# A three-stage graph layer on one core: bias in the mixing matrix, denominators among the last y products, edges six steps later, zeros from another tile

## The reference, cut to what matters

```python
xn = layernorm(x)                                  # 10,000 nodes x 512
agg = segment_sum(xn[src], dst) / max(deg, 1)      # 10,000 edges
h   = tanh(agg @ W1_l.T + xn @ W1_r.T + b1)
agg2 = segment_sum(h[src], dst) / max(deg, 1)
gnn = agg2 @ W2_l.T + h @ W2_r.T + b2
q, k, v = split(xn @ w_qkv)                        # 8 heads of 64
qp, kp = elu(q @ proj) + 1, elu(k @ proj) + 1
z   = 1 / (qp . sum_n kp)                          # one number per node and head
mix = (qp @ (kp^T v) * z) @ w_proj + b_proj
x   = x + gnn + mix
x   = x + ffn(layernorm(x))      # 8 experts, each node takes its best one
```

## Time and profile before

| | |
|---|---|
| median of 3 runs | 2788.45 us (2784.39 to 2789.29) |
| profiled execution | 2787.47 us, of which span 2785.7 us |
| mean granted TensorE clock | 0.975 |
| PE busy | 2614.7 us (94%) |
| DVE / ACT / POOL busy | 1698.5 / 987.7 / 1150.9 us |
| stage 1, first transpose to the last matmul | 26.8 to about 1022 us |
| fold and hidden | 1022 to 1519 us |
| mix, to the last product | 1519 to 2174 us |
| hand over to FFN, FFN | 2174 to 2786 us |

### The profile page before, as it was taken

How to read it: one execution, slowest core, us unless ns; L and a number is a source line. 1 busy time by engine, 2 the same in 40 slices (tenths; PEclk the granted TensorE clock), 3 DMA queues, 4 the chain that set the end, 5 groups by cost and what they waited for, 6 DMA issues and landing times.

```text
span 2785.7 us, 36335 instructions
## 1 busy us (share of the span) xinstructions
PE 2614.7 (94%) x11712; PEld 2080.2 (75%) x11712; DVE 1698.5 (61%) x3626; ACT 987.7 (35%) x1725; POOL 1150.9 (41%) x1089
## 2 busy tenths in 40 slices
PE   4899999999999989999998699999999699999999
PEld 3688888888888868888886366666667477777777
DVE  2677777777777744444443455555554477777774
ACT  2455554444444434444443222222221123223232
POOL 3577776666666630000000666666666111111110
PEclk7899999999999999999999899999999799999999
DMA  9566666455555555655665688888887323233231
GB/s 377 174 185 184 188 172 167 125 154 128 151 128 141 137 165 202 237 221 220 225 226 200 208 249 272 236 241 266 245 242 203 128 91 133 94 109 117 90 136 46
DMA packets 140309, 502.45 MB, mean 180 GB/s; under 512 B 27288, under 2 KB 27800, under 8 KB 99776
## 3 DMA queue, kind: packets, MB, share of 16 engines
q1 hardware_dynamic: 104384, 417.15, 40.2%
q0 software_dynamic: 35840, 84.23, 16.7%
HBM read 261.60 MB, written 239.73 MB: 180 GB/s over the span
## 4 chain that ended last, share of the span: by engine, by line
PE 70%; POOL 10%; issue 9%; DMA 4%; DVE 4%; ACT 1%; SPq 1%; POOLq 0%; ACTq 0%; DVEq 0%
PE bank L1158 55%; PE bank L1209 8%; POOL agg_d L360 3%; PE bank L1165 3%; POOL m_x L688 2%; DMA agg_d<-O,eidx 2%; POOL G_low L313 2%; POOL G L345 2%; DVE x2T_low L313 2%; PE bank L1345 2%; DMA agg_d<-O 1%; SPq L467 1%; PE bank L401 1%; PE bank L402 1%; ACT f_relu L847 1%
## 5 line engine op out<-in xcount | busy, mean ns | idle before, releaser
L313 POOL TENSOR_TENSOR G_low<-G,G_high 128x512 fp32r<-128x512 f32 x160 | 211.2, 1320 | 342.9 <-ACT G_high L423 342.9
L360 POOL DMA_INDIRECT agg_d<-O,eidx x160 | 273.2, 1707 | 70.1 <-issue 37.6
L345 POOL DMA_INDIRECT G<-y_d,esrc x80 | 83.3, 1041 | 494.4 <-DMA erow<-in_dst 481.9
L1005 DVE TENSOR_TENSOR m_x<-bank,m_x 128x512 f32<-128x512 f32 x80 | 55.3, 692 | 289.6 <-POOL m_x L688 263.3
L705 POOL TENSOR_SCALAR veps<-mv 128x1 f32<-128x1 f32 x80 | 26.9, 336 | 494.9 <-DVE mv L1050 494.9
L826 ACT CAST qz_high<-low 128x512 fp32r<-128x512 f32 x80 | 49.7, 621 | 395.1 <-DVE low L1018 263.7
L381 DVE SCALAR_TENSOR_TENSOR Sj<-erow,dstf,tri 128x128 f32<-128x128 int32 x160 | 162.3, 1014 | 35.5 <-DMA agg_d<-O 28.7
L390 DVE SCALAR_TENSOR_TENSOR eidx<-cnt,todump,dstf 128x1 int32<-128x1 f32 x160 | 176.6, 1104 | 8.0
L423 ACT CAST G_high<-G 128x512 fp32r<-128x512 f32 x160 | 98.9, 618 | 215.5 <-DVE G L921 196.7
L1158 PE MATMUL bank<-xnT_high,Wq_high 128*128 128x512 f32 x320 | 125.6, 393 | 28.4 <-DVE xnT_low L313 28.4
L661 POOL TENSOR_TENSOR bias<-bias,low 128x512 f32<-128x512 f32 (+1 forms) x80 | 143.5, 1794 | 0.0
(11 more groups left out here) (196 smaller groups left out, 7807.6 us busy)
## 6 DMA issues: line engine op xcount, KB each, us to landing
agg_d<-O SPq DMA_DIRECT2D x20, 1040.0 KB, 19.4
b_agg<-agg_d SPq DMA_DIRECT2D x20, 1040.0 KB, 8.4
a_x<-in_x SPq DMA_DIRECT2D x20, 1024.0 KB, 6.8
agg_d<-z_halves SPq DMA_DIRECT2D x20, 1024.0 KB, 5.7
q_d<-q_rows SPq DMA_DIRECT2D x80, 256.0 KB, 2.4
r_d<-r_rows SPq DMA_DIRECT2D x80, 256.0 KB, 3.7
r_in<-r_d SPq DMA_DIRECT2D x20, 1024.0 KB, 4.8
hT_high_d<-hT_made_high SPq DMA_DIRECT2D x20, 1024.0 KB, 10.3
```

The costliest lines, as they stand in the source:

```text
L313: return eng.tensor_tensor(out_, full, high.bitcast(F32), ALU.subtract)
L345: pool.indirect_dma_start(G[:, j, :], None, table, bass.IndirectOffsetOnAxis(ap=esrc[:, b, j:j + 1], axis=0)).then_inc(e_g[j], 16)
L360: pool.indirect_dma_start(agg, bass.IndirectOffsetOnAxis(ap=eidx[:, j, 0:1], axis=0), O[:, j, 0:width], None, compute_op=ALU.add).then_inc ...
```

## The change

- Stage 1: the zeros for agg1_d come out of a tile of their own (`zero`, in the slots of `spare`). DVE no longer waits for them; POOL does, ahead of the first scatter, and ACT ahead of the first write to `spare`, for which the weight splits from the second on stand three steps later.
- b2 and b_proj are loaded with the constants at the start and added by DVE. In the fold DVE adds bias times the first column of KS to the first 128 rows of M (`m0`), so that qz @ M holds the bias. The 80 bias adds on POOL go.
- End of hidden, start of mix: PE puts the denominators of groups 0 and 1 and the first four spreads among the last four y products; ACT does steps 0 to 4 of mix among its y copies. Steps 0 to 5 of mix are skipped in the loop proper. hT_low moves to slots 16 and 17, so that four hT loads are issued ahead of the last y store. The FFN weights move to slots 12 to 15.
- The edges run six steps behind before: `edge_steps(turn, k)` gives the edge step of step t as t-6, so gather is t-6, sum t-9, scatter t-10 against the product's t-8. On POOL a step is G_low, gather, scatter. DVE takes the multiply first, then the build, then the product's add.
- End of mix: agg2 of group 0 is loaded right after the last scatter, F2 last.

```diff
+EDGE_FROM, EDGE_EXTRA = 6, 32
...
+        zero = at("zero", 19, shape=[P, TG * AW])
...
-        mhT = [at("hT_high", 2, 2, F32R), at("hT_low", 12, 2, F32R)]
+        mhT = [at("hT_high", 2, 2, F32R), at("hT_low", 16, 2, F32R)]
...
+        mix_edges, done = [], 0
+        for t in range(32):
+            now = 0 if t < EDGE_FROM else 1 + (t % 2 if EDGE_EXTRA <= t < 32 else 0)
+            mix_edges.append([(s // 8, s % 8) for s in range(done, done + now)])
+            done += now
+        ahead = done - 32
...
+                if ph == 0 and isinstance(i, int) and i == 0:
+                    pool.wait_ge(s_z1, 16 * NG)
                 need_apart(pool, e_o, ph * NT + i + 1)
...
-            if ph == 0 and isinstance(i, int) and i == 0:
-                dve.wait_ge(s_z1, 16 * NG)
...
-        split_at = (0, 6, 12, 18, 24, 30)
+        split_at = (0, 9, 15, 21, 27, 33)
...
-                sp.dma_start(agg1_g[g], O[:, :, :].rearrange("p j w -> p (j w)")).then_inc(s_z1, 16)
+                sp.dma_start(agg1_g[g], zero[:, :]).then_inc(s_z1, 16)
...
+            for b in range(2):
+                sp.wait_ge(b_yst[b], 16 * PAIRS)
+                sp.dma_start(flat(mx_, b), x_g[b]).then_inc(m_x[b], 16)
             sp.wait_ge(b_hst, 32 * NG)
...
-                edge_scatter(pool, 1, turn, k, agg2_d.ap(), D)
-                edge_low(pool, 1, turn, k)
-                edge_gather(pool, 1, turn, k, y_d.ap())
-                if active(t, 8, NT):
...
-                    pool.tensor_tensor(xr, xr, bias[:, :], ALU.add).then_inc(m_xb, 1)
+                for te in edge_steps(turn, k):
+                    edge_low(pool, 1, *te)
+                    edge_gather(pool, 1, *te, y_d.ap())
+                    edge_scatter(pool, 1, *te, agg2_d.ap(), D)
...
+            dve.wait_ge(c_ks, 3)
+            dve.wait_ge(c_m, 1)
+            dve.scalar_tensor_tensor(m0, bias[:, :], KS[:, 0, 0:1], bank[0][:, :], ALU.mult, ALU.add
+                                     ).then_inc(c_mb, 1)
...
+            pe.wait_ge(b_hs, NT - 1)
+            denominators(0, 0)
+            pe.wait_ge(b_hl, NT - 1)
+            y_product(NG, 0)
+            denominators(0, 1)
+            y_product(NG, 1)
+            spread(0, 2)
+            spread(0, 3)
+            y_product(NG, 2)
+            spread(0, 4)
+            spread(0, 5)
+            y_product(NG, 3)
...
+            turns(pe, mix, 11, head=4, last=1, skip=6)
```

More of the change, by code:

```diff
@@ L41, in active, with turns @@
     return not isinstance(t, int) or 0 <= t - lag < count
-def turns(eng, body, tail, head=1, last=0):
-    for k in range(8 * head):
+def turns(eng, body, tail, head=1, last=0, skip=0):
+    for k in range(skip, 8 * head):
         body(k // 8, k % 8)
@@ L539, in hidden @@
                         sp.dma_start(hT_d[n][g - 1], flat(bhT[n])).then_inc(b_hst, 16)
+                    if end:
+                        sp.wait_ge(b_hst, 64)
+                        for i in range(2):
+                            for n in range(2):
+                                sp.dma_start(flat(mhT[n], i), hT_d[n][i]).then_inc(m_ht[i], 16)
+                        for i in range(2):
+                            edge_load(sp, 1, 0, i)
                     sp.wait_ge(b_yo, 4 * g)
@@ L568, in mix @@
                 first = isinstance(g, int)
-                if active(g, 1, NG) and j == 0:
+                if active(g, 1, NG) and j == 0 and not (first and g < 3):
                     turn1, b1_ = lagged(turn, b, 1, 2)
-                    need(sp, m_p, 4 * (g - 2))
+                    sp.wait_ge(m_p, 4 * (g - 2))
                     for n in range(2):
@@ L697, in mix @@
                                            ALU.mult).then_inc(s_zf, 1)
-            turns(pool, mix, 8, head=3)
+            turns(pool, mix, 11, head=4, last=1)
             pool.wait_ge(e_sc, 16 * 2 * NT)
@@ L816, in mix @@
                 t = 8 * turn + k
+                edges = edge_steps(turn, k)
+                for te in edges[0:1]:
+                    edge_high(act, 1, *te)
                 if active(t, 1, NT) and k % 4 == 1:
@@ L837, in mix @@
                              ).then_inc(s_csp, 1)
-            turns(act, mix, 9, head=3)
+            act.wait_ge(b_yst[1], 16 * (PAIRS - 1))
+            for j, steps in enumerate(((0, 1), (2, 3), (4,), ())):
+                y_out(PAIRS - 1, 1, j)
+                for k in steps:
+                    mix(0, k)
+            turns(act, mix, 11, head=4, last=1, skip=5)
             act.wait_ge(s_zf, 4)
@@ L1238, in _, with y_product @@
             pe.wait_ge(s_split, 4 * len(splits))
+            def y_product(g, j):
+                need(pe, b_yo, 4 * (g - 1) + j - 1)
+                product(bank[4 + j % 2][:, :], lambda n, c: bhT[n][:, 0, c, j * P:(j + 1) * P],
+                        lambda n, c: W2l[n][:, 0, c, :], fourth=(b_hl, 4 * g) if j == 0 else None
+                        ).then_inc(b_y, 1)
             def hidden(turn, b):
@@ L1262, in hidden, with denominators, spread @@
                                 lambda n, c: baT[n][:, 0, c, :]).then_inc(b_h, 1)
-            group_turns(pe, hidden, 1, head=2)
-            pe.wait_ge(b_yo, NT)
-            pe.wait_ge(b_hs, NT)
-            pe.wait_ge(s_w2r, 32)
-            def mix(turn, k):
-                t, b, j = 8 * turn + k, k // 4, k % 4
-                if active(t, 0, NT) and j == 0:
-                    g = 2 * turn + b
-                    pe.wait_ge(m_ph[b], 16 * (turn + 1))
-                    need(pe, m_z, g)
-                    for c in range(KC):
-                        last = pe.matmul(bank[2][0:STACK, :], KS[:, c, :], phq[b][:, 0, c, :],
-                                         start=c == 0, stop=c == KC - 1)
-                    last.then_inc(m_den, 1)
+            group_turns(pe, hidden, 0, head=2)
+            def denominators(turn, b):
+                g = 2 * turn + b
+                pe.wait_ge(m_ph[b], 16 * (turn + 1))
+                need(pe, m_z, g)
+                for c in range(KC):
+                    last = pe.matmul(bank[2][0:STACK, :], KS[:, c, :], phq[b][:, 0, c, :],
+                                     start=c == 0, stop=c == KC - 1)
+                last.then_inc(m_den, 1)
+            def spread(turn, k):
+                t = 8 * turn + k
                 if active(t, 2, NT):
@@ L1285, in mix @@
                               ).then_inc(m_zb, 1)
-                edge_pe(pe, 1, turn, k, bank[7][:, :])
+            pe.wait_ge(b_hs, NT - 1)
[10 more added lines that the diff above has]
+            y_product(NG, 3)
+            pe.wait_ge(b_yo, NT)
+            pe.wait_ge(s_w2r, 32)
+            def mix(turn, k):
+                t, b, j = 8 * turn + k, k // 4, k % 4
+                late = isinstance(t, int) and t == 8
+                if active(t, 0, NT) and j == 0 and not late:
+                    denominators(turn, b)
+                spread(turn, k)
+                edges = edge_steps(turn, k)
+                for te in edges[0:1]:
+                    edge_pe(pe, 1, *te, bank[7][:, :])
                 if active(t, 8, NT):
@@ L1298, in mix @@
                             start=False).then_inc(m_p, 1)
-            turns(pe, mix, 9, head=3)
+                if late:
+                    denominators(turn, b)
+                for te in edges[1:]:
+                    edge_pe(pe, 1, *te, bank[7][:, :])
+            turns(pe, mix, 11, head=4, last=1, skip=6)
             pe.wait_ge(s_csp, 5)
```

132 lines of the change are left out of this document (69 added, 63 removed).

## The result

| | median of runs, us | runs | range |
|---|---|---|---|
| before | 2788.87 | 4 | 2784.39 to 2789.77 |
| after | 2754.13 | 4 | 2752.09 to 2755.49 |

The ratio is 0.9878, 95% interval 0.9861 to 0.9895: 35 us faster, where 94 were forecast; the time lies outside the range given. The profiled execution took 2753.52 us, its span is 2751.7 us.

What follows compares the result with a forecast made beforehand. Bounds named: stage 1's zeros, PE's holes at mix start, and a four-engine circle through POOL's bias add costing 2.5 us a group. Savings 22 + 72 - 1 = 93 us from 2787.47 gave 2695 us, own range 2680 to 2708, wider 2676 to 2732.

Steps and rivals of the forecast that it cites:

- Stage 1, 22 us: Stage 1: PE's 28.4 us wait for the zeros goes; less late transfers, restart and broadcast loads, 22 us saved, bounds 9.5 to 29.5.
- the ring order: Stage 1: each DMA engine takes one ring's descriptors in order, so x rows cannot pass the zeros; otherwise 27 instead of 22.
- the restart at half the clock: Stage 1: a short restart of PE at half clock after the waits, 2 us lost.
- the 4 us of waiting for G_low: Stage 1: POOL's late first scatter delays G_low, so PE waits 4 us in its step 8.
- Start of mix, 36 and 23 us: Start of mix: first mix product 36 us earlier; step 9 only 23 us earlier, as third denominators wait for phi_q.
- From step 9 to the last product, 547 + 4 us: Steady mix: PE's own work of 547 us without waiting, plus 4 us allowed; 72 us saved in mix.
- The allowance of 4 us: Steady mix: 4 us allowed for single long scatters (7.5 at most) and for the 2 MB of F1.
- End of mix, -1 us: End of mix: last edge sum follows last product, FFN's first rows 14 us after it against 13.2 before; one us lost.
- (D): Rival, mix: the whole mix hangs on 80 serial scatters, slower from 8.1 us a scatter, 2810 at 8.3; chance 0.04.
- (A): Rival, steady mix: a group's pace stays, its 2.5 us hole being DMA, not the bias circle; 2744 us, chance 0.12.
- if scatters land in over 6.2 us on the median: Sign of error, mix: median scatter landing above the 6.2 us of the shortest step would show the forecast wrong.
- a group takes over 29 us: Sign of error, steady mix: groups above 29 us, where 28.3 were expected, would show the forecast wrong.

Runs made afterwards that it cites:

- two tables: Changed kernel with the mix's scatters going by turns to two tables, each waiting for the one before the last, second table not read: 2697.2 us, ratio 0.9675.
- e5: Changed kernel with the mix's hT loads cut to a sixteenth of their columns from the fourth group on: 2704.4 us, ratio 0.9699.
- e13: Changed kernel with only the x rows of a group loaded three products later, meant to be alone: 2746.0 us, ratio 0.9847.
- e14: Changed kernel with x rows loaded three products later and GpSimd's order of before (scatter, low half, gather): 2740.0 us, ratio 0.9830.
- e3: Changed kernel with GpSimd's subtraction of the mix's gathered rows cut from 512 columns to 8, the second edge-sum matmul reading G_high: 2754.3 us, ratio 0.9883.
- e1: Changed kernel with GpSimd's order in a mix step as before the change (scatter, low half, gather): 2757.0 us, ratio 0.9886.

## Why the prediction was wrong

- **Stage 1, 22 us: right.** 22.2 us by the last phi_q, 21 us by the zeros alone. First query product at 57.47 (forecast near 55), POOL's wait 11.0 us (8), DVE's on a_x 13.3 (10); PE has holes of 1.63, 1.00 and 1.32 us behind it. The x rows did come in late behind the zeros, by more than forecast, as by the ring order that the prediction weighed (DVE waits for them until 91.50, 13.5 us behind their issue). Its terms were less exact than its sum: the first query product is 2.5 us late, the holes cost 4.0 us instead of 5, and the restart at half the clock (2 us) did not come, the granted clock being 1.00 from 55 to 125 us. And without the ring order its sum would have been 23.5, not the 27 that it says, since the 4 us of waiting for G_low would have stayed.
- **Start of mix, 36 and 23 us: right.** In the times of the trace after, 22.2 us less: first mix product forecast at 1511.3, measured 1511.08; step 9 forecast at 1529.3, measured at 1530.5 (third denominators 1524.17 + 6.31 us, most of it at half the clock, after a wait of 5.07 for phi_q). There is some luck in this: from its own terms phi_q would be in at 1544 (1535.8 and 3.1 MB at 377 GB/s), not at the 1547 that it wrote, and its 1551 fits the 1544. phi_q came 2 us later than 1544 and the denominators took 1 us less than twice 3.63.
- **From step 9 to the last product, 547 + 4 us: wrong, it took 601.** This is the step that failed, and in it this sentence: "The scatters are serial: 4.9 us to landing, under the 6.2 of the shortest step." Three things in it do not hold. The 4.9 is a median, and a chain is paced by its mean; the next scatter is issued 0.75 us behind the landing, so that already before the change a step was 6.3 us on the mean, not 4.9, hidden only under the 7.7 of a step of the mix. And the 4.9 was read from a kernel in which the large transfers are issued at much the same places between the scatters in every group: 3 of 67 scatters have over 1.3 MB of them issued within 3 us. In the changed kernel 26 of 67 have, and these take 8.5 to 8.9 us on the mean: the mean landing rose from 5.5 to 6.9 us and the step to 7.7 us, against PE's 7.12 (28.47 / 4). With two tables the same stretch took 554 us, so PE's sum was right and the bound was missing. The allowance of 4 us was for "single long scatters (7.5 at most)", where 28 of 79 take longer than that; the 7.5 was the longest of 1700 to 2000 us, over the whole mix the kernel before had 10.8 as well.
- **End of mix, -1 us: wrong, -12.** In the 6.5 us between product and agg2's load I counted one scatter; as the chain has no slack, three are issued and land behind the product, one after the other, and f_xn is issued at 2147.84, 16.5 us after the product. The part and agg2 then took 8.4 us, about as forecast.
- **The sum.** 93 less 50 (601 against 551), less 1 (start of mix), less 11 (end), and 3 more from the FFN, makes 34, as in the profiled pair.
- **The rivals.** (D) had the mechanism, serial scatters, and I had it only with a pace of over 8.1 us and a chance of 0.04. Between its 8.1 and PE's 7.1 lay a case that I did not price: 7.7 us, 2754. (A) came nearest in time, 2744, for a cause that two tables exclude (DMA as the bound of a group); what spoke for it, gathers and scatters sharing the engines with the plain loads, is what makes the scatters slow. My own sign of error, "if scatters land in over 6.2 us on the median", was just met: 6.2 over the whole mix, 6.7 in the fifteen groups. The surer sign was the other, "a group takes over 29 us": 31.4.
- **What stays open.** Loads in flight make scatters slow (e5), and at the same bytes the kernels with one step of edges a step of mix lie between 2740 and 2780 us by the order of the transfers and of GpSimd's step; but whether a quite even placing reaches 28.5 us a group was not shown: e13 and e14 took one of two bursts apart and won 8 and 14 us. The runs do not part how much of a slow landing is due to the loads' bunching and how much to their total: e5 took away both. Nor is it shown why GpSimd's order is worth 38 us under one placing of the loads and nothing under another.

## What to carry to other kernels

When a bound is taken away, price the next chain by what its links cost under the new timing: a latency read from the trace of before holds for the places that transfers had there. For a chain of dependent transfers compare the mean of a whole link, landing and issue, with the bulk loads beside it, to the step of the bound engine: here 7.7 against 7.12 us, 8% over it, cost 50 us. A test that loosens the dependence (here a second table) says in one run whether the chain or the bandwidth is the limit. And before a latency is read from a view, see which instructions it counts: a median of 8.6 us here was that of two loads, not of 79 scatters.

## What the hardware showed that I had not expected

- VectorE's subtraction of 128x512 takes 0.68 us alone and 2.48 us on the mean when GpSimd's subtraction of the same size runs beside it, which itself takes 1.86 us instead of 1.29. Both are released by the landing of one scatter. That GpSimd's operation lengthens VectorE's is shown by e3, where it is 8 columns wide and VectorE's is back at 0.68. What lengthens GpSimd's is not shown: in e1 it is still 1.85 us, though VectorE's subtraction takes 0.69 there on the median. The Trainium skill, "SBUF — State Buffer", SBUF: two separate sides, says that of an operation of VectorE with two SBUF inputs and one of GpSimd that reads SBUF the first to start gets a shared pair of ports for the whole instruction, and the other is blocked. That both meet here agrees with it; by its rule the second alone would wait, for at most the length of the first, where the trace has both lengthened, by 1.80 and 0.57 us on the mean, and in the rows above it is VectorE's, the first to start (1788.65, GpSimd's G_low at 1788.80), that takes 2.54. Here it cost nothing (e3: 2754.3 us); where VectorE is the bound it would cost up to 1.8 us a tile, as an estimate from these rows.
- An accumulating scatter of 256 KB lands in 4.6 to 5 us where no large transfer is issued near it. Sorted by the plain transfers that SyncE issues within 3 us on either side of a scatter's issue, the mean landings in thirteen of the kernels are (1579 to 2100 us, classes with three or more scatters): under 0.3 MB 4.9 to 5.5 us, 0.3 to 1.3 MB 5.5 to 7.0, 1.3 to 2.3 MB 7.8 to 10.7, beyond that 8.5 to 10.5. The DMA share over the stretch says nothing of it: 0.83 with PE waiting, 0.86 with PE full.
